# Four cross-attention layers on one core: filler products on TensorE, batch 1's first products and one group of transfers moved at the program's beginning

## The chip, the core and the metric

One core of a Trainium2 chip runs the whole program. The metric is device time in microseconds (us) of that core, given as the median of several executions. A profile is one further execution, taken by the hardware profiler; its times start at the first instruction.

The engines are named as the profile does: PE is TensorE (PEld its weight loads), DVE is VectorE, ACT is ScalarE, POOL is GpSimd, SP is SyncE, which here only issues transfers. Each engine runs its own list of instructions in order, and the lists meet at semaphores.

## The reference

The reference applies four layers to `x` (4 batches of 256 rows of 256) with a context of 64 rows per batch. Layers 1 and 3 are two cross-attentions and a GELU network each, layer 2 is a cross-attention with 16 heads of 16 and a network. All of this comes after the part that the change touches. The change lies within layer 0, whose attention (with the roles of the two arguments turned in the call) lets every row of `x` look at the 64 rows of context and the 256 rows of its own batch, 320 keys in all, with 16 heads of 16 and a mask on the context keys:

```
kin  = concat([ctx_2048, x], axis=1)          # 4 x 320 x 256
q, k, v = x @ q_w + q_b, kin @ kv_w + kv_b
p    = softmax(q k^T / 4 + mask)              # per batch and head, 256 x 320
x    = x + (p v) @ out_w + out_b              # then a norm and a GELU network
```

Everything is float32, and the kernel keeps that precision where it matters by splitting a value into a rounded part and a rest.

## The kernel before, in words

Nothing is scheduled by a planner: the lists of the five engines are written out by hand in five blocks (`block.sync` at L374, `block.gpsimd` at L470, `block.tensor` at L640, `block.scalar` at L1151, `block.vector` at L1410), and the order in the code is the order on the engine.

**Layer 0 in tiles.** A step `n` (0 to 63) treats 128 queries of one batch and one pair of heads; sixteen steps are a batch, and the first eight of a batch use one half of the heads (`m = 0`), the other eight the other half (`m = 1`). A step goes through the engines: PE makes the scores (`scores(n)`, L738), DVE takes their extreme (`max0`, L1458), ACT the exponential (`exp0`, L1189), DVE the reciprocal of the sums (L1472), POOL multiplies by it (L543), PE turns the result with five transposes (`turn`, L755), DVE copies that out of PSUM (`copy0`, L1464), and after four such steps PE multiplies with the values (`values`, L766). PE's loop at L832 interleaves them: in turn `i` it does `scores(i)`, `turn(i - 3)`, every fourth turn `values(i - 7)`, and then what `aside(step, b)` puts there for the next batch.

**Keys and queries.** `base(t)` (L713) is a product of 128 columns of the key weights (even `t`) or query weights (odd `t`) with the batch's rows, `t // 4` being the batch. ACT copies it out with its bias (`base0`, L1164) into the buffer `HL`, DVE makes the rest of the split (`split0`, L1441). SP then writes keys and queries to DRAM (`spare_k`, `spare_q`) and reads them back in another layout into `K0` and `Q0`, which scores need: `spread0(b, m)` (L403) issues the two writes, the mask row, three reads for `K0` and six for `Q0`. `scores` waits for all of them at the first and the ninth step of a batch. `HL` holds one batch's values at a time, so `base0` of the next batch waits until the writes to DRAM have read it (`hl_out`, L1171).

**The beginning.** SP loads `w0` (key and query weights together), batch 0's rows of `kinT`, `cols` and three small arrays, and the value weights `vw0`; the other three batches of `kinT` come in one transfer after `spread0(0, 0)` (L437); after `spread0(0, 1)` follow the loads that POOL and the network need (`ctxT`, `ow0`, `x`, `brow`, L439 to L442, and the network's weights). POOL sets `ones` and other constants. PE does `base(0)` to `base(3)` (L826), the values of batch 0 (`values_of`, L723), then the loop. For batch 1, `aside` puts `base(4)` behind `scores(0)` with a wait for `kinT` (L795), and `base(5)` behind `scores(2)`. On ACT and DVE the matching `base0` and `split0` stand behind the first and third step in the same way (L1255, L1528).

Of the kernel before, what the change touches and what calls it, by code (L numbers as in the profile page):

```python
# [25 lines left out]
P = 128  # L26
# [80 lines left out]
def build(nc, t):  # L107
    ctx = ExitStack()
    with ctx:
# [120 lines left out]
        in_base = sem("in_base")  # L230
        in_w1 = sem("in_w1")
# [18 lines left out]
        hl_out = [sem(f"hl_out{i}") for i in range(2)]  # L250
        in_k0 = [sem(f"in_k0_{i}") for i in range(2)]
# [121 lines left out]

        @block.sync  # L374
        def _(sp):
            sp.dma_start(w0, t["w0"]).then_inc(in_base, 16)
            sp.dma_start(kinT[:, :, 0, :], t["kinT"][:, :, 0, :]).then_inc(in_base, 16)
            sp.dma_start(cols[:, :], t["cols"]).then_inc(in_vec, 16)
# [3 lines left out]
            sp.dma_start(arena[:, 10752:11264].rearrange("p (d n) -> p d n", d=DH), t["vw0"]).then_inc(in_vw0, 16)  # L382

# [19 lines left out]
            def spread0(b, m):  # L403

                q = 2 * b + m
                for w, (spare, at) in enumerate(((spare_k, slice(0, KEYS0)), (spare_q, slice(KEYS0, KEYS0 + S)))):
                    sp.wait_ge(hl_ready, 2 * q + w + 1)
                    sp.dma_start(spare[b, m].rearrange("c p n -> p c n"), HL[:, m, :, at].bitcast(F32))\
                        .then_inc(hl_out[w], 16)
# [12 lines left out]
                sp.wait_ge(hl_out[1], 16 * (q + 1))  # L422
                for block, part in enumerate((0, 0, 1)):
                    for e in range(2):
                        at = 32 * block + 16 * e
                        sp.dma_start(Q0[at:at + 16, m, :, e, :].bitcast(F32),
                                     spare_q[b, m, part].rearrange("(j e q) n -> e q j n", j=4, e=2)[e])\
                            .then_inc(in_q0[m], 16)
# [8 lines left out]
            sp.dma_start(kinT[:, :, 1:B, :], t["kinT"][:, :, 1:B, :]).then_inc(in_kin, 16)  # L437
# [203 lines left out]
        def _(pe):  # L641
# [68 lines left out]
            def attend0():  # L710
                N = TILES * PAIRS

                def base(t):  # L713

                    b, m, w = t // 4, t // 2 % 2, t % 2
                    if t == 1:
                        pe.wait_ge(w0_scaled, 1)
                    for d in range(DH):
# [72 lines left out]
                def aside(step, b):  # L791
# [3 lines left out]
                    if step == 0 and more:  # L795
                        pe.wait_ge(in_kin, 16)
                        pe.wait_ge(v0_ready, 3 * b + 3)
                        base(t)
                    elif step == 2 and more:
# [31 lines left out]
                pe.wait_ge(consts_ready, 1)  # L831
                for i in range(N + 4):  # L832
# [284 lines left out]

            pe.wait_ge(in_base, 32)
# [33 lines left out]
        def _(act):  # L1152
# [11 lines left out]
            def base0(t):  # L1164
# [4 lines left out]
                if b >= 1:  # L1169

                    act.wait_ge(hl_out[w], 16 * (2 * (b - 1) + m + 1))  # L1171
# [73 lines left out]
            for t in range(4):  # L1245
                base0(t)
            act.wait_ge(consts_ready, 1)
            for j in range(3):
                values_of0(0, j)
# [161 lines left out]
        def _(dve):  # L1411
# [38 lines left out]
            for t in range(4):  # L1450
                split0(t)
# [430 lines left out]
```

## Time and profile before

| | us |
|---|---|
| median of 3 runs | 957.06 (953.86 to 961.48) |
| profiled execution, first to last instruction | 957.6 |
| scores of step 0 start | 18.36 |
| scores of step 8 start | 41.97 |
| PE busy in the whole span | 881.7 (92%) |

The page of the profile gives only the span of the profiled execution, not a time of its own with what lies around it; the span is within 0.6 us of the median of the runs. The trace has one row per instruction or per run of equal instructions: its start, its length, its engine and line, what it writes and reads, and, in brackets, how long its engine had been idle before it and what ended that. A float32 product appears as two rows of the engine. The row "PEclk" and the column of that name give the clock that TensorE was granted, 1.00 being 2.4 GHz and 0.50 being 1.2 GHz.

### The profile page before, as it was taken

To read this page: it belongs to the slowest core of one execution; us is meant where nothing else is said; L and a number is where in the kernel's file an instruction comes from. 1 tells how busy PE (TensorE), PEld (TensorE's weight loads), DVE (VectorE), ACT (ScalarE), POOL (GpSimd) and SP (SyncE) were. 2 spreads that over 40 slices of the span, in tenths; PEclk is the share of its full clock that TensorE was granted. 3 is DMA by queue.
4 is the path that set the end of the run, shared out by engine and by line. 5 is a ranking of instruction groups with operands and counts; after the bars stand their busy time and mean duration, and the time that the engine had idled before them with its cause. 6 is when DMAs were issued, how large, how long until landed. Compare 5 with 4: busy or idle time off the path is not lost.

```text
span 957.6 us, 15739 instructions
## 1 busy us (share of the span) xinstructions
PE 881.7 (92%) x5624; PEld 737.2 (77%) x5624; DVE 604.0 (63%) x1344; ACT 491.8 (51%) x1205; POOL 484.3 (51%) x507
## 2 busy tenths in 40 slices
PE   4889876899999999999899898899999999999898
PEld 3677755899966789666797787899975689757788
DVE  3688887416779757796423545325779867798440
ACT  2566655654753356533663332764763347632662
POOL 2667876474543345465293170184544335465383
PEclk8699999999999999999999988999999999999999
DMA  6823312002550025200002000101570015200001
GB/s 188 294 91 87 102 38 96 5 2 72 168 213 1 1 70 162 100 1 0 23 2 88 1 2 0 64 37 40 160 254 0 1 35 164 67 1 1 1 12 34
DMA packets 26673, 64.04 MB, mean 67 GB/s; under 512 B 2995, under 2 KB 15843, under 8 KB 25444
## 3 DMA queue, kind: packets, MB, share of 16 engines
q1 hardware_dynamic: 26596, 63.03, 20.2%
q8 instruction: 46, 0.75, 0.3%
q14 instruction: 31, 0.25, 0.1%
HBM read 57.22 MB, written 5.77 MB: 66 GB/s over the span
## 4 chain that ended last, share of the span: by engine, by line
PE 70%; DVE 19%; issue 5%; POOL 3%; ACT 1%; DMA 1%; SPq 1%; DVEq 0%; POOLq 0%
PE ps L964 7%; PE ps L904 6%; PE ps L863 6%; PE ps L865 6%; PE ps L893 5%; PE ps L940 4%; PE ps L762 3%; PE ps L705 3%; PE ps L706 3%; PE ps L707 3%; PE ps L686 3%; DVE prob L1658 3%; PE ps L687 3%; PE ps L688 3%; DVE mx L1657 3%
## 5 line engine op out<-in xcount | busy, mean ns | idle before, releaser
L964 PE MATMUL ps<-arena,pT_all 128*128 128x256 f32 x512 | 116.6, 381 | 5.7 <-DVE x L1678 3.6
L964 PEld LDWEIGHTS ps<-arena,pT_all 128*128 128x128 f32 x512 | 96.2, 190 | 32.3 <-issue 15.1
L940 PE MATMUL ps<-arena,hT 128*128 128x512 f32 x256 | 115.5, 594 | 0.0
L536 POOL TENSOR_TENSOR rstd<-var,neg_half 128x1 f32<-128x1 f32 (+1 forms) x56 | 33.9, 606 | 155.1 <-DVE var L1487 155.1
L543 POOL TENSOR_TENSOR arena<-arena,rinv 128x640 f32<-128x640 f32 x64 | 80.4, 1257 | 55.4 <-DVE rinv L1472 55.3
L570 POOL TENSOR_TENSOR prob<-prob,rinv 128x512 f32<-128x512 f32 x32 | 49.5, 1547 | 113.2 <-DVE rinv L1671 113.2
L1196 ACT ACTIVATE arena<-ps,nb 128x320 f32<-128x320 f32 x128 | 66.4, 523 | 58.1 <-DVE nb L1458 57.9
L1239 ACT ACTIVATE arena_r<-ps,cols 128x256 fp32r<-128x256 f32 x128 | 66.5, 520 | 55.1 <-PE ps L688 55.0
L512 POOL TENSOR_TENSOR vacc<-vacc,vpart 128x256 f32<-128x256 f32 x60 | 44.0, 734 | 98.6 <-ACT vpart L1311 98.3
L589 POOL TENSOR_TENSOR arena_r<-arena,arena_r 128x512 fp32r<-128x512 f32 x64 | 83.9, 1333 | 13.2 <-ACT arena L1240 13.2
L686 PE MATMUL ps<-hH,w1H 128*128 128x256 f32 x256 | 75.2, 294 | 11.9 <-DVE prob L1658 5.1
L940 PEld LDWEIGHTS ps<-arena,hT 128*128 128x128 f32 x256 | 46.1, 190 | 46.8 <-issue 45.9
L1343 ACT ACTIVATE prob<-prob 128x512 f32<-128x512 f32 x32 | 20.2, 630 | 116.0 <-DVE prob L1658 116.0
L705 PE MATMUL ps<-w2H,arena_r 128*128 128x256 f32 x256 | 72.5, 283 | 1.6 <-DVE x L1574 1.6
L687 PE MATMUL ps<-hL,w1H 128*128 128x256 f32 x256 | 73.2, 286 | 0.0
L688 PE MATMUL ps<-hH,w1L 128*128 128x256 f32 x256 | 73.1, 286 | 0.0
L762 PE MATMUL ps<-ident,arena 128*128 128x128 f32 x320 | 50.1, 291 | 24.4 <-DVE pT_all L1464 12.1
L706 PE MATMUL ps<-w2L,arena_r 128*128 128x256 f32 x256 | 72.0, 281 | 0.0
L707 PE MATMUL ps<-w2H,arena_r 128*128 128x256 f32 x256 | 71.8, 281 | 0.0
L1458 DVE TENSOR_REDUCE nb<-ps 128x2 f32<-128x640 f32 x64 | 52.4, 819 | 28.8 <-PE ps L751 28.7
L503 POOL TENSOR_TENSOR u<-ring,lnb 128x256 f32<-128x256 f32 x64 | 67.7, 1057 | 0.0
L893 PE MATMUL ps<-HL,wq 128*128 128x256 f32 x384 | 67.3, 311 | 0.0
(164 smaller groups left out, 2350.9 us busy)
## 6 DMA issues: line engine op xcount, KB each, us to landing
ring<-in_heads_dram SPq DMA_DIRECT2D x64, 512.5 KB, 3.6
w<-in_w_dram SPq DMA_DIRECT2D x8, 1024.0 KB, 7.3
first_r<-spare_k SPq DMA_DIRECT2D x24, 160.0 KB
first_q<-spare_q SPq DMA_DIRECT2D x48, 64.0 KB, 2.6
spare_k<-HL SPq DMA_DIRECT2D x8, 320.0 KB, 2.4
spare_q<-HL SPq DMA_DIRECT2D x8, 256.0 KB, 2.3
x<-in_x_dram SPq DMA_DIRECT2D x1, 1024.0 KB, 6.0
lnb<-in_lnb_dram SPq DMA_DIRECT2D x4, 256.0 KB, 6.6
```

The source lines that it names most:

```text
L543: g.tensor_tensor(w, w, rinv[:, n % 2, 0:2].unsqueeze(2).broadcast_to([P, 2, KEYS0]), ALU.mult)\
L589: g.tensor_tensor(hidL[:, (b + 1) % 2, two, :], hid[:, (b + 1) % 2, two, :], hidH[:, b % 2, two, :].bitcast(F32), ALU.subtract).then_inc(h ...
L686: mm(o, w1H[:, d, block], hH[:, k, d, :], start=(d == 0), stop=False)
L687: mm(o, w1H[:, d, block], hL[:, k, d, :], start=False, stop=False)
L688: last = mm(o, w1L[:, d, block], hH[:, k, d, :], start=False, stop=(d == 1))
L705: mm(o, hidH[:, k, f, at], w2H[:, f, :], start=(f == 0), stop=False)
L706: mm(o, hidH[:, k, f, at], w2L[:, f, :], start=False, stop=False)
L707: last = mm(o, hidL[:, 1 - k, f, at], w2H[:, f, :], start=False, stop=(f == FT - 1))
L762: last = nc.tensor.transpose(ps[:, 4 + c // 4, (c % 4) * P:(c % 4 + 1) * P], prob0[:, n % 4, c * P:(c + 1) * P], ident[:, :])
L893: last = mm(ps[:, 2 + k, d * B * C:(d + 1) * B * C], wq[:, k, c, d * P:(d + 1) * P], KT[:, k, e, :], start=(p == 0), stop=(p == 2))
L940: last = mm(ps[:, SCORES[k][half], :], hT[:, k, d, 0:P], A[:, d, b // 2, cols_of, sl, :].rearrange("p r s k -> p r (s k)"), start=(d == 0) ...
L964: last = mm(ps[:, 6, 0:D], pT[:, k, c, :], VW[:, b, c, :], start=(c == 0), stop=(c == PAIRS - 1))
```

## The change

On PE, a helper `keep_warm(n, cols)` multiplies the constant `ones` with itself into a PSUM bank that holds nothing yet. It is called twice: nine products of 128 columns before the wait for the first inputs, and eight of 256 columns directly before the loop of steps. `base(4)` and `base(5)` stand before the second call and no longer behind `scores(0)` and `scores(2)`; for that, batch 1's rows of `kinT` are loaded early by themselves.

```diff
@@ tensor
+                    if t == 4 or t == 8:
+                        pe.wait_ge(in_kin, 4 * t)
...
-                    if step == 0 and more:
-                        pe.wait_ge(in_kin, 16)
+                    if step == 0 and more and b >= 1:
                         pe.wait_ge(v0_ready, 3 * b + 3)
                         base(t)
-                    elif step == 2 and more:
+                    elif step == 2 and more and b >= 1:
                         pe.wait_ge(hl_ready, t + 1)
                         base(t + 1)
...
                 pe.wait_ge(consts_ready, 1)
+                pe.wait_ge(hl_ready, 4)
+                base(4)
+                pe.wait_ge(hl_ready, 5)
+                base(5)
+                keep_warm(8, D)
                 for i in range(N + 4):
...
+            def keep_warm(n, cols):
+
+                for _ in range(n):
+                    mm(ps[:, 6, 0:cols], ones[:, :], ones[:, :].unsqueeze(1).broadcast_to([P, cols // P, P]),
+                       start=True, stop=True)
+
+            pe.wait_ge(pool_set, 1)
+            keep_warm(9, P)
             pe.wait_ge(in_base, 32)
             attend0()
```

On SP, `w0` is loaded in two halves with the rows of `kinT` between them, and DVE's scaling of the query half waits for that half alone (`in_w0q`). `kinT` of batch 1 is loaded right behind `vw0`, that of batches 2 and 3 at the old place. The six reads into `Q0` of `spread0(0, 0)` move from SP to ACT, where they stand behind `base0(3)` and wait for the write of the queries (`q_out`); `base0` and `split0` of `t = 4, 5` move ahead of the first step on ACT and DVE.

```diff
@@ sync
-            sp.dma_start(w0, t["w0"]).then_inc(in_base, 16)
+            sp.dma_start(w0[:, 0, :, :], t["w0"][:, 0, :, :]).then_inc(in_base, 16)
             sp.dma_start(kinT[:, :, 0, :], t["kinT"][:, :, 0, :]).then_inc(in_base, 16)
+            sp.dma_start(w0[:, 1, :, :], t["w0"][:, 1, :, :]).then_inc(in_w0q, 16)
...
+            sp.dma_start(kinT[:, :, 1, :], t["kinT"][:, :, 1, :]).then_inc(in_kin, 16)
...
-                        .then_inc(hl_out[w], 16)
+                        .then_inc(q_out if q == 0 and w == 1 else hl_out[w], 16)
...
+                if q > 0:
+                    sp.wait_ge(hl_out[1], 16 * q)
+                    spread_q(sp, b, m)
...
-            sp.dma_start(kinT[:, :, 1:B, :], t["kinT"][:, :, 1:B, :]).then_inc(in_kin, 16)
+            sp.dma_start(kinT[:, :, 2:B, :], t["kinT"][:, :, 2:B, :]).then_inc(in_kin, 16)
@@ scalar
             for t in range(4):
                 base0(t)
+            act.wait_ge(q0_set, 1)
+            act.wait_ge(q_out, 16)
+            spread_q(act, 0, 0)
             act.wait_ge(consts_ready, 1)
             for j in range(3):
                 values_of0(0, j)
+            base0(4)
+            base0(5)
@@ vector
-            dve.wait_ge(in_base, 32)
+            dve.wait_ge(in_w0q, 16)
             v.tensor_scalar(w0[:, 1, :, :], w0[:, 1, :, :], -1.0 / HD, None, ALU.mult).then_inc(w0_scaled, 1)
...
-            for t in range(4):
+            for t in range(6):
                 split0(t)
```

`spread_q` is the old loop over six reads as a function of the issuing engine. The list of PE before, from the end of batch 0's values to the fourth step's scores (each step's scores are two products of 320 columns, `L719` is `base`):

```order
L735 MATMUL ps<-arena 64x128
L751 MATMUL ps<-first_r,first_q 128x320 [waits in_k0_0,in_q0_0,row_set,consts_ready]
L751 MATMUL ps<-first_r,first_q 128x320
L719 MATMUL ps<-arena 128x320 [waits v0_ready,in_kin]
L719 MATMUL ps<-arena 128x320
L751 MATMUL ps<-first_r,first_q 128x320 [waits v0_ready]
L751 MATMUL ps<-first_r,first_q 128x320
L751 MATMUL ps<-first_r,first_q 128x320 [waits p0_ready]
L751 MATMUL ps<-first_r,first_q 128x320
L719 MATMUL ps<-arena 128x256 [waits hl_ready]
L719 MATMUL ps<-arena 128x256
L751 MATMUL ps<-first_r,first_q 128x320 [waits p0_ready]
```

The same place of PE with the change (`base` is now at L729, `scores` at L761, the filler at L1135):

```order
L745 MATMUL ps<-arena 64x128
L729 MATMUL ps<-arena 128x320 [waits in_kin,hl_ready,consts_ready]
L729 MATMUL ps<-arena 128x320
L729 MATMUL ps<-arena 128x256 [waits hl_ready]
L729 MATMUL ps<-arena 128x256
L1135 MATMUL ps<-ones 128x256 x8
L761 MATMUL ps<-first_r,first_q 128x320 [waits in_q0_0,in_k0_0,row_set]
L761 MATMUL ps<-first_r,first_q 128x320
L761 MATMUL ps<-first_r,first_q 128x320 [waits v0_ready]
L761 MATMUL ps<-first_r,first_q 128x320
L761 MATMUL ps<-first_r,first_q 128x320 [waits p0_ready]
```

The four products of batch 1 and the eight of filler now stand ahead of every score, and the second pair of them waits for a split that DVE makes from ACT's copy. On ACT, the list from batch 0's last copy to the first exponential reads with the change (L1197 is `base0`, L1205 to L1209 the copies of the values, L1219 `exp0`):

```order
L1197 ACTIVATE HL<-ps,qb0 128x256 [waits base_ps]
L380 DMA first_q<-spare_q 16x4x256 [waits q_out,q0_set]
L380 DMA first_q<-spare_q 16x4x256 x5
L1205 ACTIVATE arena<-ps 128x16x16 [waits v0_ps,consts_ready]
L1205 ACTIVATE arena<-ps 128x16x16 [waits v0_ps]
L1208 ACTIVATE arena<-ps 64x8x16 [waits v0_ps]
L1209 ACTIVATE arena<-ps 64x8x16
L1197 ACTIVATE HL<-ps,cols 128x320 [waits hl_out0,base_ps]
L1197 ACTIVATE HL<-ps,qb0 128x256 [waits base_ps]
L1219 ACTIVATE arena,sm<-ps,nb 128x320 [waits nb_ready]
```

Before, the six rows of transfers were not on ACT, and the two rows of `base0` stood behind the first and the third step's exponentials. Now the first of these two, which PE's `base(5)` waits for through DVE, stands behind the six issues and the four copies.

## Rows read from the trace of the kernel before

**Rows 1.** The page: length of the span, and TensorE's granted clock in 40 slices.

```profile
span 957.6 us, 15739 instructions
PEclk8699999999999999999999988999999999999999
```

**Rows 2.** Timeline of PE and PEld, 0 to 43 us: start, length, instruction, idle before.

```profile
5.37 7.02 PE L719 MATMUL ps<-arena 128*128 128x320 f32 x16 [5.37 <-DMA arena<-in_kinT_dram]
10.44 0.34 PEld L719 LDWEIGHTS ps<-arena 128*128 128x128 f32 x1 [0.20 <-issue]
18.36 0.87 PE L751 MATMUL ps<-first_r,first_q 97*128 97x320 f32 x2 [3.59 <-DMA first_q<-spare_q]
22.26 2.50 PE L719 MATMUL ps<-arena 128*128 128x320 f32 x4 [3.03 <-DMA arena<-in_kinT_dram]
41.97 0.56 PE L751 MATMUL ps<-first_r,first_q 97*128 97x320 f32 x2
```

**Rows 3.** Five stretches: length, busy time of each engine, PEclk, DMA share.

```profile
18.20:22.00 3.80, 0.87 (x2) 0.50 (x2) 0.82 (x1) 1.13 (x4) 0.00 (x0) 0.50 0.90 276
25.00:41.50 16.50, 13.58 (x79) 10.83 (x81) 10.70 (x21) 8.70 (x30) 10.84 (x10) 0.50 0.95 336
...
156.00:160.00 4.00, 2.30 (x16) 1.87 (x17) 3.76 (x8) 2.75 (x10) 3.24 (x3) 1.00 0.00 0
161.80:164.50 2.70, 1.06 (x9) 0.82 (x8) 1.01 (x2) 2.13 (x5) 1.23 (x1) 1.00 0.96 347
165.00:168.00 3.00, 2.89 (x13) 2.92 (x14) 0.01 (x1) 0.58 (x1) 0.00 (x0) 0.50 0.83 323
```

**Rows 4.** The chain that ended last, two pieces: start, length, what.

```profile
16.06 6.16 DMA arena<-in_kinT_dram
...
64.54 0.86 PE ps L719 x4
```

**Rows 5.** Timeline of DVE: constants, first split, score extremes of steps 3, 8, 57, 63.

```profile
6.75 0.17 DVE L1431 TENSOR_SCALAR qb<-cols 128x2 f32<-128x2 f32 x1 [0.95 <-DMA bo<-in_bo_dram]
8.54 0.55 DVE L1446 SCALAR_TENSOR_TENSOR HL<-ps,cols,HL 128x320 fp32r<-128x320 f32 x1 [0.40 <-ACT HL L1174]
...
29.37 0.82 DVE L1458 TENSOR_REDUCE nb<-ps 128x2 f32<-128x640 f32 x1 [1.86 <-PE ps L751]
...
42.57 0.82 DVE L1458 TENSOR_REDUCE nb<-ps 128x2 f32<-128x640 f32 x1 [1.96 <-PE ps L751]
...
148.51 0.81 DVE L1458 TENSOR_REDUCE nb<-ps 128x2 f32<-128x640 f32 x1
...
159.53 0.81 DVE L1458 TENSOR_REDUCE nb<-ps 128x2 f32<-128x640 f32 x1
```

**Rows 6.** Timeline of ACT, 9 to 16 us: the first query copy, the value copies.

```profile
9.62 0.47 ACT L1174 ACTIVATE HL<-ps,qb 128x256 fp32r<-128x256 f32 x1 [1.11 <-PE ps L719]
...
14.28 0.66 ACT L1182 ACTIVATE arena<-ps 128x256 f32<-128x256 f32 x2 [1.37 <-PE ps L730]
...
15.10 0.27 ACT L1186 ACTIVATE arena<-ps 64x128 f32<-64x128 f32 x1
```

**Rows 7.** Timeline of SP's issues: value weights, first queries written, then read back.

```profile
3.65 0.36 SPq L382 DMA_DIRECT2D arena<-in_vw_dram  x1
...
10.63 0.37 SPq L408 DMA_DIRECT2D spare_q<-HL  x1
...
13.24 2.77 SPq L426 DMA_DIRECT2D first_q<-spare_q  x6
```

**Rows 8.** Transfers issued 10 to 16 us: size each, us from issue to landing.

```profile
spare_q<-HL SPq DMA_DIRECT2D x1, 256.0 KB, 2.1
first_q<-spare_q SPq DMA_DIRECT2D x6, 64.0 KB, 2.9
```

**Rows 9.** Timeline of POOL: `ones` set, and the addition behind the fifth step's product.

```profile
0.72 0.21 POOL L473 MEMSET ones<- 128x128 f32 x1 [0.29 <-POOLq L1868]
...
36.10 0.73 POOL L488 TENSOR_TENSOR arena<-x,brow 128x256 f32<-128x256 f32 x1 [0.28 <-DMA brow<-in_brow_dram]
```

More of the change, by code:

```diff
@@ L230, in build @@
         in_base = sem("in_base")
+        in_w0q = sem("in_w0q")
         in_w1 = sem("in_w1")
@@ L250, in build @@
         hl_out = [sem(f"hl_out{i}") for i in range(2)]
+        q_out = sem("q_out")
         in_k0 = [sem(f"in_k0_{i}") for i in range(2)]
@@ L371, in build, with spread_q @@
         SEQ = (0, 1, 3, 4)
+        def spread_q(eng, b, m):
+            for block, part in enumerate((0, 0, 1)):
+                for e in range(2):
+                    at = 32 * block + 16 * e
+                    eng.dma_start(Q0[at:at + 16, m, :, e, :].bitcast(F32),
+                                  spare_q[b, m, part].rearrange("(j e q) n -> e q j n", j=4, e=2)[e])\
+                        .then_inc(in_q0[m], 16)
         @block.sync
         def _(sp):
-            sp.dma_start(w0, t["w0"]).then_inc(in_base, 16)
+            sp.dma_start(w0[:, 0, :, :], t["w0"][:, 0, :, :]).then_inc(in_base, 16)
             sp.dma_start(kinT[:, :, 0, :], t["kinT"][:, :, 0, :]).then_inc(in_base, 16)
+            sp.dma_start(w0[:, 1, :, :], t["w0"][:, 1, :, :]).then_inc(in_w0q, 16)
             sp.dma_start(cols[:, :], t["cols"]).then_inc(in_vec, 16)
@@ L421, in spread0 @@
                                  spare_k[b, m, part].rearrange("(j q) n -> q j n", j=4)).then_inc(in_k0[m], 16)
[L422 to L428, printed above, removed]
+                if q > 0:
+                    sp.wait_ge(hl_out[1], 16 * q)
+                    spread_q(sp, b, m)
             sp.wait_ge(q0_set, 1)
@@ L1169, in base0 @@
                 if b >= 1:
-                    act.wait_ge(hl_out[w], 16 * (2 * (b - 1) + m + 1))
+                    if w == 0 or t > 5:
+                        act.wait_ge(hl_out[w], 16 * (2 * (b - 1) + m + 1 - w))
                 if t == 1:
@@ L1254, in _ @@
                 if b + 1 < B:
-                    if step in (0, 2, 8, 10):
+                    if step in (8, 10) or (b >= 1 and step in (0, 2)):
                         base0(4 * (b + 1) + (0, 2, 8, 10).index(step))
@@ L1527, in _ @@
                     invert0(i - 1)
-                if step in (1, 3, 9, 11) and b + 1 < B:
+                if b + 1 < B and (step in (9, 11) or (b >= 1 and step in (1, 3))):
                     split0(4 * (b + 1) + (1, 3, 9, 11).index(step))
```

## The prediction

> **What bounds the kernel now.** I read the page first: the span is 957.6 us, and the row of the granted clock is full but for the first slices and a few later ones [rows 1]. So the change can only act in about the first 42 us, and what it gains there must be carried as a shift through the rest. Next the timelines of the engines over this stretch. The reader should see four things. TensorE starts its products at 5.37, when the first inputs have landed [rows 2]. It then does nothing for 3.59 us until the scores of step 0 at 18.36, which waited for the transferred queries [rows 2]. Behind step 0 it waits another 3.03 us for batch 1's inputs and then makes `base(4)` in 2.50 us [rows 2]; the chain of waits charges 6.16 us to that transfer [rows 4]. So step 1 really begins at 24.8, and step 8 at 41.97 [rows 2]. Last the granted clock: it is at the lower level (1.2 GHz) from the end of the pause until past 41.5 and at the upper one later [rows 3]. Up to the pause the column reads 1.00, but the first sixteen records take 7.02 us, 0.44 each [rows 2], twice the 0.215 of a later `base` (four in 0.86 [rows 4]), and a weight load at 10.44 still takes 0.34 us [rows 2]; so I read that the engine also began at the lower level and rose after that load.
>
> I take step 8's scores (41.97) as the mark: from there on both kernels have the same work, and what is gained by then is the change of the time.
>
> **The first filler** (nine products, 18 records) can start when `ones` is set at 0.93 [rows 9]. A 256-column product costs 0.43 us at the upper clock, since `base` with two of them takes 0.86 [rows 4]; 128 columns cost half, 0.21, or 0.43 at the lower clock. So it takes 1.9 to 3.9 us and ends by 4.9, before or with the landing of the inputs; it costs nothing as long as they do not land before 4.4. What it brings is a clock that rises some us earlier, so that `base(0)` to `base(3)` and the values end at about 11 instead of 14.8. Little of that reaches the path: DVE's constants begin only at 6.75, when the last small array has landed, and end at 8.14, 0.40 before the first split [rows 5]. Splitting `w0` puts one more issue (0.36, like that of the value weights [rows 7]) ahead of these arrays. The first key split stays at 8.5 to 8.6 and ends near 9.1. I count zero for the keys, and between -0.4 and +0.4 as bounds.
>
> **The queries' way** gains. Their copy on ACT starts at 9.62 now because of a 1.11 us wait for PE [rows 6]; with the quicker products the split can follow the keys' at once and the write is issued at about 9.8 instead of 10.63 [rows 7]. It lands 2.1 us later [rows 8], at 11.9. ACT is free by then and issues the six reads at once. On SP they took 2.77 us together [rows 7] and began at 13.24, behind those for the keys. No row shows an issue from ACT. Bounds: almost nothing (an engine that only hands it over), and twice SP's time; I take SP's 2.77, the same kind of instruction. The reads are issued by 14.7 and, at 2.9 us to landing [rows 8], there by 17.6.
>
> The Trainium skill ("DMA: Bandwidth & Descriptors", section "Issuing engines are not separate DMA queues") says that issuing from several engines saves only the issue time, which it calls usually small beside the transfer. Here the trace differs on "small": 2.77 us of issues stand against 2.9 us to landing. By that page the sharing of the transfer engines remains, so SP's loads, now issued at the same time, can hold the queries up; 17.6 would be a lower bound.
>
> **What the issues are in front of.** On ACT, the copies of the values (14.28 to 15.37, 1.09 us [rows 6]) and then `base0(4)` stand behind the six issues. So: issues end 14.7, copies 15.8, `base0(4)` 16.3 (0.5, after 0.47 for 256 columns [rows 6]), split 16.9 (0.55 [rows 5]). Only then may PE do `base(5)`: 0.86 at the upper clock [rows 4], to 17.8. And then the second filler: eight products of 256 columns, four times 0.86 = 3.4 us, to 21.2. The scores of step 0 come after that, although keys and queries are there at 17.6. So step 0 starts later than the 18.36 of before, and step 1 earlier than 24.8, because the 3.03 us wait, the 2.50 us and the second product are gone from between.
>
> **The steps.** Without products of another batch between them, six steps at the upper clock take 159.53 - 148.51 = 11.0 us [rows 5], 1.84 each; eight are 14.7. POOL's additions of 0.73 [rows 9] from the fifth step on make it some 15.2. Step 8 starts at 21.2 + 15.2 = 36.4, which is 5.5 earlier than 41.97.
>
> Something is late next: POOL's addition at step 4 waits for `brow` even now, 0.28 us at 36.10 [rows 9]. SP comes to that load at most 2.8 us earlier (six issues fewer), while the step comes about 4 earlier. That takes up to 1.2 us; I count 0.6. Gain 4.9.
>
> **The gap in PE's work.** Between `base(4)` (over at 12 to 13.5) and `base(5)` (17) PE has nothing. A pause of 3.59 us was followed by the lower clock [rows 2, 3]. This one is about as long, so I give even chances that the clock falls. Then `base(5)` and filler run at half speed until it rises; dense work from 165 on was still at the lower clock for 3 us [rows 3], the first work of the program from 5.37 until after 10.44, 5 us [rows 2]; I take 3 to 6 us. Half of 8.6 us of work at the lower clock and the rest at the upper one puts step 0 at 23 to 24.2, step 8 at 39 and the gain at 3. The mean of both ways is 4, so 957.06 - 4 = 953.
>
> **Moved without price.** Filler writes a bank that nothing holds yet, on an engine that waits. SP loses six issues and gains two (0.36 and some 0.6); its second group of keys and queries is there by about 27, and step 8 wants it at 36. Batch 1's split lies ready in the buffer earlier; its transfers stay behind the network's weights.
>
> **Rivals.**
>
> *The clock falls in the first steps.* Steps 0 to 3 bring only scores until the first transposes. If the clock is at the lower level after the filler, the steps go as they did: steps 3 to 8 took 42.57 - 29.37 = 13.2 us [rows 5], with about 4.5 for the three before, 17.7 in place of 15.2. Step 8 comes at 39 to 41.5, and the time is 955. Against it: 156 to 160 has 2.30 us of scores and transposes in 4.0 and keeps the clock [rows 3]. For it: in 161.8 to 164.5 PE worked 1.06 of 2.7 us, on nine transposes, and at 165 the clock was at the lower level [rows 3]. The Trainium skill ("TensorE: Matmul & The Clock Gate", "Part 4: PE-mode transpose") says that transposes do not count as activity for the clock; those nine agree with it, and by that rule the first steps would be poorer still. Chance 0.22.
>
> *The filler is in the way: slower.* Where the clock falls in the gap and does not rise before the scores, the filler costs 6.9 and step 0 starts at 17 + 1.7 + 6.9 = 25.6; with 17.7 for the steps, step 8 starts at 43.3, 1.3 later than now. If an issue from ACT costs twice SP's, that is another 2.8 and some us: 961. The point from which it decides is step 0's start: beyond 24.3 with slow steps, beyond 26.8 with fast ones, the change loses. I price it at 960, chance 0.13.
>
> *The issues cost ACT almost nothing.* Then everything behind them is 2.5 us earlier, the gap closes, step 0 starts at 18.8 and step 8 at 34 (`brow` then holds POOL for longer): 950, chance 0.07.
>
> **The numbers.** Forecast 953 with 0.58: the upper clock in the first eight steps. The three runs of before lie within 0.8% (957.06, with 953.86 and 961.48), so 1% is about what a measurement can tell, and 1% is 9.6 us. No case above reaches it; only scatter does. The range takes in 950 and 960 and the runs' scatter at the lower end: 947.5 to 960. Faster by over 1%: 0.06; slower: 0.03; within: 0.91.
>
> **What would show it.** In the profile after: PE's first row at about 1 us; the six issues on ACT from 11.9 to 14.7; a pause of 3.5 to 5 us in PE before `base(5)`; the second filler in 3.4 us (clock up) or up to 6.9; step 0's scores at 21 to 24, step 8's at 36 to 39; the clock at 1.00 between these. I am wrong if step 0 starts before 20 or after 25, if the steps go at 2.3 us each, or if the gain at step 8 is gone by the last step (64 steps, the network), which would mean a wait there for something that did not move along.

## The result, and the profile after

The changed kernel takes 959.4 us (median of 20 runs) against 956.15 of the kernel before in the same comparison: ratio 1.0038, interval 1.0021 to 1.0054. It is slower by 3.3 us by the medians and by some 3.6 by the ratio, where 953 and a gain were forecast. It is the rival "the filler is in the way" (960), though not for its reasons alone.

The timeline of PE in the changed kernel (start, length, instruction, idle before) answers to [rows 2]; the last row is step 8.

```profile
0.98 4.21 PE L1135 MATMUL ps<-ones 128*128 128x128 f32 x18 [0.98 <-POOL ones L481]
5.60 4.89 PE L729 MATMUL ps<-arena 128*128 128x320 f32 x16 [0.41 <-DMA arena<-in_kinT_dram]
12.79 1.34 PE L729 MATMUL ps<-arena 128*128 128x320 f32 x4
19.22 2.07 PE L729 MATMUL ps<-arena 128*128 128x256 f32 x4 [5.08 <-DVE HL L1474]
21.08 5.16 PE L1135 MATMUL ps<-ones 128*128 128x256 f32 x16
25.89 0.94 PE L761 MATMUL ps<-first_r,first_q 97*128 97x320 f32 x4
...
34.58 1.30 PE L772 MATMUL ps<-ident,arena 128*128 128x128 f32 x5 [0.48 <-DVE pT_all L1492]
...
36.89 1.30 PE L772 MATMUL ps<-ident,arena 128*128 128x128 f32 x5 [0.47 <-DVE pT_all L1492]
...
42.72 0.90 PE L761 MATMUL ps<-first_r,first_q 97*128 97x320 f32 x2
```

The first filler does what it should: the sixteen records of the keys and queries end at 10.5, not 12.4. But `base(5)` comes at 19.22 after a pause of 5.08 us, the second filler takes 5.16 us, step 0 starts at 25.89, and the steps then go at 2.31 us (34.58 to 36.89). Step 8 begins at 42.72, 0.75 later than before [rows 2], although `base(4)` and `base(5)` are out of its way.

What held `base(5)` is on ACT (the second row is ACT's queue, six issues; the last is DVE's split, which `base(5)` waits for):

```profile
7.92 0.53 ACT L1197 ACTIVATE HL<-ps,cols 128x320 fp32r<-128x320 f32 x1 [5.70 <-DMA bo<-in_bo_dram]
...
12.98 3.85 ACTq L380 DMA_DIRECT2D first_q<-spare_q  x6
16.93 0.66 ACT L1205 ACTIVATE arena<-ps 128x256 f32<-128x256 f32 x2 [5.93 <-issue]
...
18.05 0.53 ACT L1197 ACTIVATE HL<-ps,cols 128x320 fp32r<-128x320 f32 x1
...
18.61 0.55 DVE L1474 SCALAR_TENSOR_TENSOR HL<-ps,cols,HL 128x320 fp32r<-128x320 f32 x1 [7.09 <-ACT HL L1197]
```

The copy of `base(4)` stands behind the six issues and the copies of the values; only when it is split (18.61 to 19.16) may `base(5)` run. The granted clock over the same stretches (length, busy time by engine, PEclk, DMA share) answers to [rows 3]:

```profile
12.00:17.00 5.00, 2.14 (x15) 1.18 (x13) 0.00 (x0) 0.07 (x1) 0.00 (x0) 1.00 0.89 196
18.00:24.00 6.00, 4.78 (x11) 3.87 (x12) 1.03 (x2) 1.03 (x3) 0.00 (x0) 0.50 0.72 238
24.50:30.50 6.00, 3.71 (x19) 2.71 (x18) 2.88 (x6) 2.56 (x9) 1.55 (x2) 1.00 0.86 273
31.50:44.00 12.50, 10.96 (x73) 8.59 (x74) 7.57 (x14) 5.23 (x20) 8.31 (x8) 0.50 0.91 327
```

The clock is at the lower level for `base(5)` and for most of the filler that should have kept it up, at the upper one when the scores begin, and lower again from 31 until past 44, through the scores of steps 4 to 8.

DVE's rows of the score extremes answer to [rows 5]: step 8 at 43.66 (42.57 before), the last step at 162.32 (159.53):

```profile
43.66 0.82 DVE L1486 TENSOR_REDUCE nb<-ps 128x2 f32<-128x640 f32 x1 [2.30 <-PE ps L761]
...
162.32 0.81 DVE L1486 TENSOR_REDUCE nb<-ps 128x2 f32<-128x640 f32 x1
```

The spans of the two profiled executions (957.2 and 957.6) do not show the loss: between 560 and 590 us the mean granted clock is 0.94 in this one and 0.83 in that of before, which gives some 3 us back in this one execution. So the times below are medians of many runs, and of the profiles (one for each kernel) I use only the beginning, as far as step 9: from there to step 50 the lead or lag of each kernel to the kernel before stays the same within 0.2 us (experiment 4 alone loses another 1.5 by step 12).

### The profile page after: what moved, and what is told of

Read it like the earlier page. It is cut to its first block, busy times and chain, and to the rows that moved or that the text cites. A ratio compares the mean times of both kernels' runs of the same rounds, so it can differ in the third digit from the quotient of the medians.

```text
span 957.2 us, 15807 instructions
## 1 busy us (share of the span) xinstructions
PE 885.6 (93%) x5658; PEld 741.9 (78%) x5658; DVE 603.9 (63%) x1344; ACT 491.1 (51%) x1205; POOL 484.1 (51%) x507
## 4 chain that ended last, share of the span: by engine, by line
PE 70%; DVE 19%; issue 5%; POOL 3%; ACT 2%; DMA 1%; ACTq 0%; SPq 0%; DVEq 0%; POOLq 0%
PE ps L978 7%; PE ps L918 6%; PE ps L877 6%; PE ps L879 6%; PE ps L907 5%; PE ps L954 4%; PE ps L772 4%; PE ps L713 3%; PE ps L714 3%; PE ps L715 3%; PE ps L694 3%; DVE prob L1686 3%; PE ps L695 3%; PE ps L696 3%; DVE mx L1685 3%
## 5 line engine op out<-in xcount | busy, mean ns | idle before, releaser
L978 PEld LDWEIGHTS ps<-arena,pT_all 128*128 128x128 f32 x512 | 96.3, 190 | 32.3 <-issue 15.2
L544 POOL TENSOR_TENSOR rstd<-var,neg_half 128x1 f32<-128x1 f32 (+1 forms) x56 | 33.8, 604 | 152.1 <-DVE var L1515 152.1
L1219 ACT ACTIVATE arena<-ps,nb 128x320 f32<-128x320 f32 x128 | 66.3, 523 | 57.7 <-DVE nb L1486 57.7
L1263 ACT ACTIVATE arena<-ps,cols 128x256 f32<-128x256 f32 x128 | 66.9, 522 | 0.0
```

What stands on the lines that cost most here:

```text
L978: last = mm(ps[:, 6, 0:D], pT[:, k, c, :], VW[:, b, c, :], start=(c == 0), stop=(c == PAIRS - 1))
```

## The experiments

All are compared with the kernel before, run on the same chip; 9, 10 and 12 have 5 or 6 runs, the others 10 to 20. "Step 0" is the start of its scores, "step 9" the start of its extreme on DVE (44.49 in the profile of before), "brow" POOL's wait for that load.

| kernel | step 0 | brow | step 9 | median us | ratio, interval |
|---|---|---|---|---|---|
| changed kernel | 25.89 | 0 | 46.16 | 959.4 | 1.0038 (1.0021 to 1.0054) |
| 1 reads on SP | 21.39 | 3.56 | 40.51 | 954.66 | 0.9989 (0.9965 to 1.0013) |
| 2 no second filler | 21.44 | 1.11 | 38.61 | 955.52 | 0.9994 (0.9972 to 1.0016) |
| 3 before + first filler | 17.00 | 0.99 | 40.09 | 955.37 | 0.9985 (0.9954 to 1.0016) |
| 4 = 1 and 2 | 17.42 | 6.58 | 41.26 | 955.89 | 0.9976 (0.9948 to 1.0004) |
| 5 copies ahead of issues | 22.61 | 0.94 | 43.03 | 956.9 | 0.9998 (0.9976 to 1.002) |
| 6 filler in the gap | 21.68 | 1.96 | 42.50 | 954.29 | 0.9983 (0.9956 to 1.0011) |
| 7 = 4, products in the steps | 17.81 | 7.23 | 42.17 | 956.69 | 0.9996 (0.9975 to 1.0017) |
| 8 before + reads on ACT | 21.80 | 1.22 | 43.45 | 957.26 | 1.0008 (0.9979 to 1.0038) |
| 9 = 7, additions later | 18.57 | 0 | 35.16 | 951.55 | 0.9938 (0.9917 to 0.9958) |
| 10 = 4, additions later | 17.98 | 0 | 37.74 | 952.61 | 0.9949 (0.9931 to 0.9968) |
| 11 before, additions later | 18.31 | 0 | 41.39 | 956.26 | 0.9997 (0.9973 to 1.0021) |
| 12 = 1, additions later | 19.52 | 0 | 36.32 | 953.0 | 0.9953 (0.9933 to 0.9973) |
| 13 changed, additions later | 25.07 | 0 | 45.40 | 959.36 | 1.0051 (1.0031 to 1.007) |
| 14 = 10, no filler at all | 17.85 | 0 | 38.04 | 951.32 | 0.9959 (0.9934 to 0.9984) |
| 15 = 2, additions later | 22.27 | 0 | 39.44 | 956.26 | 0.9995 (0.9968 to 1.0021) |
| 16 = 15, reads undisturbed | 19.25 | 0 | 39.80 | 954.09 | 0.9957 (0.9931 to 0.9984) |

### Which part of the change costs (1 to 4)

1, the six reads by SP again:

```diff
-                if q > 0:
-                    sp.wait_ge(hl_out[1], 16 * q)
-                    spread_q(sp, b, m)
+                sp.wait_ge(hl_out[1] if q > 0 else q_out, 16 * max(q, 1))
+                spread_q(sp, b, m)
...
-            spread_q(act, 0, 0)
```

> The changed kernel with the six reads of the first queries issued by SP again (behind those of the keys), the rest as changed. Theory 'front': step 0 started at 25.9 because TensorE's base(5) stood behind ACT's six issues (3.85 us) and then 5.2 us of filler ran half at the lower clock. Then base(5) follows base(4) at once, no gap, clock up, filler 3.4 us, step 0's scores at 18 to 19.5, step 8 at 34 to 38, about 950 to 953 us. Rival 'clock': what costs is the pace of the steps at the lower clock, which fell again at 31; then step 0 comes earlier but the clock falls in the first steps again, 2.3 us each, step 8 at 37 to 38, 953. Rival 'transfers': sharing of the transfer engines is what delays step 0; then its scores wait for first_q or first_r, and start after 20.

2, without the second filler, and 4, both edits together:

```diff
-                keep_warm(8, D)
```

> The changed kernel without the second filler (eight products of 256 columns). Front: step 0's scores right behind base(5), at about 21; the clock has fallen in the gap and stays low, steps at 2.3; step 8 at 39 to 41, 4 to 6 us before the changed kernel's 45.5; about 954 us. Clock: the filler keeps the first five us of the steps quick; without it the steps are slower by what step 0 gains, and the time stays at 959.

> Queries' reads on SP and no second filler: both parts undone. Front: step 0 when its queries have landed, 18 to 19; a pause of 3 to 4 us before it may let the clock fall; step 8 at 34 to 37; 950 to 953, within 1 us of the kernel with the filler. Clock: the filler's use shows here: without it the steps go at 2.3 from the start and it is 2 to 3 us slower than with the queries on SP and the filler kept.

3, the kernel before with the first filler only:

```diff
+            pe.wait_ge(pool_set, 1)
+            for _ in range(9):
+                nc.tensor.matmul(ps[:, 6, 0:P], ones[:, :], ones[:, :], start=True, stop=True)
```

> The kernel before with only the first filler (nine products of 128 columns ahead of the wait for the first inputs). Front: base products end some 2 us earlier, queries are written 0.5 to 1 us earlier, step 0 up to 1 us earlier, but step 1 still waits for batch 1's inputs at 22.2, which come at most 1 us earlier: 0 to -1 us against before. Clock: the same, since the pause before step 0 still lets the clock fall: 0.

Each of 1 and 2 alone brings back 4 to 5 us: 954.66 and 955.52 lie at the kernel before, with intervals that hold 1. PE in 1, where ACT is free:

```profile
17.15 1.13 PE L728 MATMUL ps<-arena 128*128 128x256 f32 x4 [1.21 <-DVE HL L1471]
18.12 3.62 PE L1134 MATMUL ps<-ones 128*128 128x256 f32 x16
21.39 0.93 PE L760 MATMUL ps<-first_r,first_q 97*128 97x320 f32 x4
```

Without the pause the same `base(5)` takes 1.13 and the same filler 3.62. Step 0 still misses the 18 to 19.5 of the theory "front": it stands behind the filler, not behind a transfer, and the steps then go at 2.3 us, as the rival "clock" had it. In 2 step 0 (21.44) came as expected; the steps were quicker than that, since the clock rose within them at 29.6. So the pause, the low clock and the filler are one loss: the reads on ACT make the pause, and the clock that falls in it makes what follows dear.

In 3 step 0 comes 1.4 us earlier than before, and nothing that can be told is left of it in the time. So none of the four is clearly faster than the kernel before, and 4 is the puzzle: its step 0 starts 8.5 us before that of the changed kernel and 0.9 before that of the kernel before, its step 8 nearly 7 us earlier, and yet its time gains only 0.24%, with an interval that holds 1. Something later takes it back.

### ACT's order, the gap, the steps, the reads alone (5 to 8)

5, the copies of the values and of `base(4)` ahead of ACT's issues:

```diff
-            spread_q(act, 0, 0)
             act.wait_ge(consts_ready, 1)
             for j in range(3):
                 values_of0(0, j)
             base0(4)
+            spread_q(act, 0, 0)
             base0(5)
```

> The changed kernel, with ScalarE's copies of the values and base0(4) put ahead of its six issues (base0(5) behind them). Theory 'the issues stand in front of the copies': base(5) no longer waits for 5.08 us; it runs by about 14.5, the second filler ends at 18 to 19 at the upper clock, the queries are issued from 13.5 to 17.4 and are there at about 20.5, step 0 starts there (25.9 in the changed kernel), step 8 at 37 to 39 (43.7): 3 to 5 us less than the changed kernel, 955. Rival 'an issue from ScalarE is too slow wherever it stands': the six reads land after 23, step 0 starts after 23 and no more than 2 us come back: 957 to 959. In both, steps of 2.3 us if the clock falls again after the filler.

ACT's queue, and then PE, in 5:

```profile
13.38 4.02 ACTq L380 DMA_DIRECT2D first_q<-spare_q  x6
```

```profile
14.49 1.13 PE L729 MATMUL ps<-arena 128*128 128x256 f32 x4 [1.20 <-DVE HL L1474]
15.46 3.62 PE L1135 MATMUL ps<-ones 128*128 128x256 f32 x16
22.61 0.82 PE L761 MATMUL ps<-first_r,first_q 97*128 97x320 f32 x4 [3.53 <-DMA first_q<-spare_q]
```

Half of each theory: `base(5)` comes at 14.49 as the first said, but the queries are there only at 22.61, 5.2 us after the last issue. The rival's mark was 23. ACT's issues were not only in front of copies; what they issued came late.

6, the second filler between `base(4)` and `base(5)`:

```diff
                 base(4)
+                keep_warm(8, D)
                 pe.wait_ge(hl_ready, 5)
                 base(5)
-                keep_warm(8, D)
```

> The changed kernel, with the second filler between base(4) and base(5), in the wait of 5.08 us, in place of behind base(5). Theory 'gap, clock and filler one behind the other': the filler (3.4 us at the upper clock) ends at about 17.6 and costs nothing, the clock does not fall before base(5) at about 19.2, which takes 0.9 to 1.1 in place of 2.07; step 0 starts at 20.5 to 21.5 (25.9), step 8 at 37 to 39 (43.7): about 955. Rival 'the clock of the first steps is all that counts': step 0 earlier, but the steps at 2.3 us and the low clock reaching further: 957 or more.

Step 0 (21.68) and the median (954.29) lie near what was expected, but again PE ends up waiting for the queries, 2.27 us. With the pause filled the clock held through it, and `base(5)` took 1.13; it fell at 20.5, in the wait for the queries, and the steps went at 2.31 us, so that step 8's extreme came at 40.02 and not at 37 to 39. On the steps the rival was right.

7, products of `ones` among the steps, with 4's other edits:

```diff
                         aside(i % 16, i // 16)
+                    if 1 <= i <= 6:
+                        keep_warm(2, D)
```

> Queries issued by SP, no second filler, but two 256-column products of ones behind each of the steps 1 to 6. It was 955.89 without them, with the clock at the lower level from 16.0 to 46.6, steps of 2.3 us, step 8's maximum at 35.76. Theory 'the first steps lack work for the clock': the clock is up again within a few steps, steps 4 to 7 take 1.75 to 1.9 us, step 8's maximum comes at 33 to 34 and no slow steps follow it: 952 to 953. Rival 'the products are in the way': 0.43 to 0.86 us more in each step with the clock low, step 8's maximum at 37 to 40, 957 to 959.

This run shows the second cause. DVE's extremes of steps 7, 8 and 9, then POOL's row between the last two:

```profile
30.38 0.82 DVE L1484 TENSOR_REDUCE nb<-ps 128x2 f32<-128x640 f32 x1 [0.34 <-PE ps L760]
32.70 0.82 DVE L1484 TENSOR_REDUCE nb<-ps 128x2 f32<-128x640 f32 x1 [0.70 <-PE ps L760]
42.17 0.82 DVE L1484 TENSOR_REDUCE nb<-ps 128x2 f32<-128x640 f32 x1 [1.84 <-PE ps L760]
```

```profile
36.15 0.72 POOL L495 TENSOR_TENSOR arena<-x,brow 128x256 f32<-128x256 f32 x1 [7.23 <-DMA brow<-in_brow_dram]
```

PE's stretch of the steps in 7 (length, busy time by engine, PEclk, DMA share):

```profile
24.00:32.00 8.00, 7.85 (x82) 6.62 (x80) 7.11 (x13) 5.14 (x19) 3.72 (x3) 1.00 0.85 260
```

The clock theory holds for the pace: at 1.00 from 24 to 32, steps 4 to 7 take 1.7 to 2.0 us and step 8 comes at 32.70, 9.9 us before that of the kernel before. Then POOL, which puts its addition of `brow` behind step 4's product, stands 7.23 us for that load, everything behind POOL stands, and step 9 comes at 42.17. Of 9.9 us 2.3 are left, and the time does not change. The wait also puts PE into a pause (5.48 us), after which its clock was at the lower level again.

8, the reads on ACT as the only edit of the kernel before (`spread_q(act, 0, 0)` behind ACT's first four copies, no reads by SP for the first group):

> The kernel before, with only the first six reads of the queries issued by ScalarE in place of SP; no filler, batch 1's products where they were. Theory 'the issue from ScalarE costs more and holds up': the reads are issued from about 13 to 16.9 in place of 13.24 to 16.0, step 0 starts 0.5 to 1.5 us later (18.4 in the kernel before), 957.5 to 958.5. Rival 'SP's six issues less bring more': the transfer of the other batches' inputs is issued 2.8 us earlier, the wait of 3.03 us for base(4) goes, step 8's maximum comes 1 to 3 us before 42.57: 954 to 956.

ACT's queue, and then PE's step 0, in 8:

```profile
12.70 2.76 ACTq L379 DMA_DIRECT2D first_q<-spare_q  x6
```

```profile
21.80 0.87 PE L756 MATMUL ps<-first_r,first_q 97*128 97x320 f32 x2 [7.14 <-DMA first_q<-spare_q]
```

Issued 0.5 us earlier and in no more time than on SP [rows 7], the reads land 3.4 us later than SP's: step 0 at 21.80, not 18.36. Neither theory had this. Step 8's extreme comes at 41.03, 1.5 us earlier, as the rival said, but not its gain in time: that is the same within the interval. SP's other loads come earlier, and `base(4)` no longer waits, against the late step 0.

### The load that did not move (9 to 14)

9, 10, 11 and 12 are 7, 4, the kernel before and 1, each with POOL's eight additions eight steps later (their results are first used in step 21):

```diff
-                if n == 4:
+                if n == 12:
                     pool.wait_ge(in_w0, 16 * 4)
-                if 4 <= n < TILES + 4:
-                    add_row(x0, n - 4, "L0_out_b")
+                if 12 <= n < TILES + 12:
+                    add_row(x0, n - 12, "L0_out_b")
```

> The kernel with queries issued by SP, no second filler and two products of ones behind each of the steps 1 to 6, with POOL's eight additions of brow moved from steps 4 to 11 to steps 12 to 19. Without the move step 8's maximum came at 32.70, and POOL then waited 7.23 us for brow, so that step 9's maximum came at 42.17. Theory 'brow's landing is the floor': the wait goes, step 9's maximum comes at 34.5 to 36.5 (44.49 in the kernel before), 6 to 8 us less than in the kernel before: 948 to 951. Rival 'another load is the floor' (the second group of keys and queries, the other batches' inputs) or 'given back by the low clock in steps 9 to 16': step 9 after 38, or the 6 us gone by step 16: 954 to 957.

> The kernel with queries issued by SP and no second filler, with POOL's additions of brow at steps 12 to 19 in place of 4 to 11. Step 8's maximum was at 35.76 and step 9's at 41.26, behind a wait of 6.58 us for brow. Theory 'brow's landing is the floor': step 9's maximum at 37.5 to 39, the clock up before 44, 4 to 6 us less than the kernel before: 951 to 953. Rival: the low clock holds until 46 as it did and takes it back: 955 to 956, as without the move.

> The kernel before, with POOL's additions of brow at steps 12 to 19 in place of 4 to 11, and nothing else. There POOL waited only 0.28 us for brow, and reached the addition at 35.8, when brow had all but landed. Theory 'brow's landing bounds only a start that comes earlier': no change within 1 us: 956 to 957. Rival 'the additions themselves (eight of 0.73 us) stand in POOL's way in the slow steps': 2 to 4 us less: 953 to 955.

> The changed kernel with the first queries issued by SP, second filler kept, with POOL's additions of brow at steps 12 to 19 in place of 4 to 11. It was 954.66 with the additions early; POOL waited 3.56 us for brow, while step 8's maximum came at 38.59. Theory 'brow's landing is the floor': the wait was partly hidden by steps of 2.3 us, 1 to 2 us come back: 952.5 to 954. Beside the kernel without the second filler and with the same move it shows what the filler is worth when brow is out of the way: theory 'the filler only delays step 0' says 1 to 3 us slower than that one; rival 'the clock it holds up pays for it' says no slower.

DVE's extremes of steps 7, 8 and 9 in experiment 9:

```profile
30.94 0.82 DVE L1484 TENSOR_REDUCE nb<-ps 128x2 f32<-128x640 f32 x1 [0.33 <-PE ps L760]
33.25 0.82 DVE L1484 TENSOR_REDUCE nb<-ps 128x2 f32<-128x640 f32 x1 [0.69 <-PE ps L760]
35.16 0.82 DVE L1484 TENSOR_REDUCE nb<-ps 128x2 f32<-128x640 f32 x1 [0.30 <-PE ps L760]
```

The hole of 9.5 us between 8 and 9 is gone. All four went as the theory said: POOL waits no longer, 9 and 10 reach step 9 at 35.16 and 37.74, and the times of 10, 11 and 12 lie in its ranges, that of 9 lies 0.5 us above. By the medians the move is worth 5.1 us in 9 (against 7), 3.3 in 10 (against 4) and 1.7 in 12 (against 1), by the ratios 0.58, 0.27 and 0.36%: most where the wait for `brow` was longest (7), the only one of the three beyond the intervals by itself, and nothing in the kernel before (11: 0.9997). These three are the first that are clearly faster than the kernel before. Experiment 12 against 10 leaves the second filler without an effect that can be told (953.0 and 952.61), and 9 against 10 the products within the steps (0.9938 and 0.9949): they bring step 8 earlier in the profile, but any gain in time is within the scatter.

13, the changed kernel with the same move, and 14, experiment 10 without the first filler as well:

> The changed kernel with POOL's additions of brow at steps 12 to 19 in place of 4 to 11, nothing else. Theory 'the changed kernel loses by its late step 0 (25.9), and brow holds nothing there': POOL did not wait for brow in it, so at most the additions' own place in the slow steps comes back: 0 to 2 us less, 957.5 to 959.5, not faster than the kernel before. Rival 'brow is the floor here too': 4 us or more come back, 955 or less.

> No filler at all, the first queries issued by SP, batch 1's first products ahead of the first scores, the additions of brow at steps 12 to 19. With the first filler it was 952.61. Theory 'the first filler carries the early products': without it base(0) to base(3) take 7 us again, base(5) ends at about 18 in place of 15.5 and step 0 starts 1.5 to 2.5 us later: 954 to 955. Rival 'the transfers set step 0 and the filler is idle work': step 0 within 0.7 us of 18, 952 to 953.

13 stays where it was (959.36): the changed kernel is so late that `brow` is there before it. So its own loss is not one of `brow`. With the reads on SP the move brings a clear gain (9, 10 and 12); in 2, with the reads on ACT, it gains nothing (15 below). 14 went the rival's way. Its PE:

```profile
5.54 5.82 PE L728 MATMUL ps<-arena 128*128 128x320 f32 x16 [5.54 <-DMA arena<-in_kinT_dram]
...
16.20 1.13 PE L728 MATMUL ps<-arena 128*128 128x256 f32 x4 [1.20 <-DVE HL L1468]
17.85 0.82 PE L760 MATMUL ps<-first_r,first_q 97*128 97x320 f32 x4 [0.52 <-DMA first_q<-spare_q]
```

Without any filler `base(5)` is 1.8 us later than with one (14.39 in 10), and still ahead of the queries, which set step 0 at 17.85. Its median is the lowest (951.32), but by its ratio (0.9959) it can't be told from 9, 10 and 12. Beside 11 (0.9997) it shows what the rest of the change is worth without fillers, without reads on ACT and with `brow` out of the way: batch 1's loads and products ahead of the first scores bring some 0.4%, though the two intervals still touch.

### Why the queries land late (15, 16)

15 is 2 with the additions later, the control. 16 lets SP wait until the queries have landed:

```diff
             spread0(0, 0)
+            sp.wait_ge(in_q0[0], 96)
             sp.dma_start(kinT[:, :, 2:B, :], t["kinT"][:, :, 2:B, :]).then_inc(in_kin, 16)
```

> The changed kernel without the second filler and with POOL's additions of brow at steps 12 to 19: what is left of ScalarE's reads when neither the filler nor brow stands behind them. With the reads on SP it was 952.61. In the four runs with the reads on ScalarE that show it, TensorE got the first queries at 21.4 to 22.6, with SP at 17.4 to 18.6. Theory 'the reads on ScalarE land late': step 0 at about 21.4 again, 3 us behind the kernel with the reads on SP, 955 to 956. Rival 'the place of the reads no longer matters': 952 to 953.

> The same, and SP waits until the first queries have landed before it issues the load of the other batches' inputs and the writes of the second group. Theory 'SP's later transfers, issued at the same time, hold ScalarE's reads up': with the transfer engines to themselves the six reads land 2.5 to 3.5 us after their issue in place of 5.6 to 6.1, at 18 to 19.5, and step 0 starts there (unless base(5), behind ScalarE's copies, comes later, at 18 to 20). Rival 'reads issued by ScalarE take longer by themselves': they land 5 us or more after issue also alone, step 0 at 21 or later. The time says less, since the second group of keys and queries comes 3 to 5 us later.

Transfers issued from 8 to 30 us (size of each, median from issue to landing), first in 15:

```profile
arena<-in_kinT_dram SPq DMA_DIRECT2D x1, 640.0 KB, 7.4
...
first_q<-spare_q ACTq DMA_DIRECT2D x6, 64.0 KB, 5.7
```

and in 16, with SP's first issue behind its wait, from its timeline:

```profile
arena<-in_kinT_dram SPq DMA_DIRECT2D x1, 640.0 KB, 5.0
...
first_q<-spare_q ACTq DMA_DIRECT2D x6, 64.0 KB, 3.4
```

```profile
17.95 0.62 SPq L446 DMA_DIRECT2D arena<-in_kinT_dram  x1
```

Alone, the six reads land after 3.4 us, near SP's 2.9 [rows 8]; SP goes on at 17.95, so they are there by then, and step 0 starts at 19.25 behind `base(5)`, in place of 22.27. The issue from ACT is not slow by itself. SP, freed of the six reads, issues the 640 KB of the other batches' inputs and two writes of together 576 KB while ACT's reads are still under way, and they share the transfer engines. On SP's own queue the reads had gone ahead of those. Both expectations came in: 15 stays at the kernel before (0.9995), and 16 is faster (0.9957), although its profile reaches step 9 no earlier than that of 15.

## Why the prediction was wrong

**The sum.** Step 8's scores were forecast at 36.4, or at 39 with the clock falling in the gap, and came at 42.72. Of these 6.3 us, 4.7 are step 0 (25.89, not 21.2) and 1.6 the steps (16.8, not 15.2). What failed is the path to step 0: the chain in front of `base(5)` was priced 2.3 us too short, the clock fell in the pause that the chain makes, and `base(5)` and the second filler then ran mostly at the lower level. The even chances for the gap put the forecast between two cases of a gain; the third case, the filler in the way, had 0.13, and slow steps by themselves 0.22.

**The first filler: right, and without worth.** It ran from 0.98 to 5.19 (4.21, a little over the bound of 3.9), was over 0.41 us before the inputs landed, and the products behind it ran faster. I counted zero for the keys; the split came at 9.25, 0.7 later than before, since the small arrays landed at 7.9 (6.75 before [rows 5]) behind the split load of `w0`, more than the bound of 0.4; in all fourteen kernels with the split load they landed at 7.06 to 7.92, in the four without it at 6.50 to 6.75. Experiment 14 shows that the time the filler saves lies ahead of a transfer that ends later anyway.

**The start of step 1.** Its scores began at 24.09 in the kernel before, not at 24.8; no term of the sum uses this.

**The queries' way: mis-sized, and hidden here by the filler.** The write was issued at 10.27 (9.8 foreseen) and landed 2.6 us later (2.1). The issues took 3.85 (2.77; between 2.76 and 4.02 in the runs, so the price from SP's row was the low end). The landing is where the term was wrong: 5.7 us after issue, not 2.9. The price came from a row in which SP's reads ran ahead of the large load in the same queue [rows 7, 8], and the change itself takes them out of that order. Queries at 17.6 were forecast; where PE waits for them in a kernel with the large load alongside, it is 21.4 to 22.6. The sentence on the Trainium skill ("DMA: Bandwidth & Descriptors", "Issuing engines are not separate DMA queues") had said it: the sharing of the engines remains, and 17.6 was a lower bound. The trace agrees, by 3.8 to 5 us, and experiment 16 shows it. I had written that as a remark and given it no price. In the changed kernel this error does not show: step 0's row names no wait, since the filler ends later than the queries land. It is the next limit as soon as the filler is out of the way (2, 5, 6 and 15).

**What the issues are in front of: right in kind, too short, and the first term on the path that failed.** The chain of issues, value copies, copy and split of `base(4)` was foreseen link by link, with `base(5)` at 16.9; it came at 19.22, late by 1.1 at the reads' start, 1.1 in the issues and the rest in between.

**The gap.** I gave even chances that the clock falls; at 5.08 us of pause it fell, with 2.07 and 5.16 in place of 0.86 and 3.4. In experiment 6, where the filler stands in the pause, it held until 20.5. The price of this case was right: 23 to 24.2 for step 0, with `base(5)` 2.2 later than the 17 counted there, is 25.2 to 26.4. Step 0's 25.89 is the rival's 25.6 (which I gave 0.13), and beyond its turning point of 24.3 for slow steps.

**The steps: wrong.** The forecast needed the upper clock through the first eight steps, but after the filler it fell at 31. Experiment 1 has the same (step extremes 2.31 us apart, 29.84 to 32.15) with a filler that ran at the upper clock, and in 12 the clock fell at 24 in the same way. The fillers ahead of the steps did not hold the clock; products of `ones` within them did (7 and 9). But steps without any also brought it up, at 29.6 in 2 and at 30.4 in 15 (and at 29.2 in 3 and 31.0 in 11, with batch 1's products among them). Two stretches of 2, in which PE did nothing but scores and transposes from 21.44 until past 34 (length, busy time by engine, PEclk, DMA share):

```profile
27.00:28.00 1.00, 1.00 (x4) 0.50 (x2) 0.82 (x3) 1.00 (x5) 0.96 (x2) 0.50 0.92 373
...
32.00:33.00 1.00, 0.56 (x6) 0.59 (x6) 1.00 (x3) 0.44 (x2) 0.68 (x1) 1.00 1.00 367
```

The Trainium skill has the rule that transposes do not count as activity ("TensorE: Matmul & The Clock Gate", "Part 4: PE-mode transpose"). That rule alone does not explain these runs: steps of the same scores and transposes lost the clock in the changed kernel and raised it in 2. The nine transposes of the prediction do not bear it out either: PE stood still for 2.25 us behind them before its next row at the lower level, at 165.11. Why the clock fell in the one kernel and rose in the other stays open.

**What is late next: named, and mis-sized.** I put the wait for `brow` at up to 1.2 and counted 0.6. It lands at 33.8 to 36.2 in every kernel that waited for it, whatever else changes, because it is issued at 26.2 to 28.7, behind the second group of keys and queries. That is a floor under step 4's addition: it cost up to 7.2 us. So a step 8 in time was not enough for the forecast's gain: experiment 1 starts step 8's scores at 37.99, within the forecast's 36 to 39, and its time is 0.11% below the kernel before, with an interval that holds 1.

**One limit.** The loss of 3.3 to 3.6 us is larger than the 1.7 us by which step 9 lags in the two profiles, and than the 2.8 at layer 0's last step. Experiment 11, equal to the kernel before in its time, has the same lists on all engines up to POOL's first addition; yet its clock was up from 31.0 and not from 41.9, and it comes to step 9 at 41.39, 3.1 us earlier. Of this lead it gives 2.6 us back between steps 50 and 60, with the clock at the lower level from 147.0 to 153.8. So the clock rises and falls at other moments in two executions of equal work, by as much as most differences here. How the loss divides between the beginning and later stretches was not measured.

## What to carry to other kernels

A transfer's time from issue to landing belongs to its place in a queue: when an issue moves to another engine, ask what the first engine will now issue alongside it, and price the landing with that. Before making a beginning faster, look for the load that the first slower consumer waits for (here an addition of a bias, on an engine with time to spare) and move that consumer: it cost nothing here, and with the reads on SP it decided whether anything earlier was a gain. Filler for the clock paid nowhere here: ahead of the steps it did not hold the clock, behind a wait it stood in the way, and within the steps it held the clock without a gain in time beyond the scatter. Where the clock moves by itself from one execution to the next, compare many runs and not two profiles.

## What was not expected of the hardware

The column of the granted clock reads 1.00 from the start, but the sixteen records of the keys and queries took 7.02 us in the kernel before [rows 2] and 4.15 in experiment 3, which differs up to there only by the filler: the column is not to be trusted ahead of its first change. And six issues of the same form on ACT took between 2.76 and 4.02 us in different kernels, with single ones of up to 1.42 us against 0.45; on SP they took 2.77 in nearly every one.
